# Three f16 products in place of an f32 product in the second and third feed-forward of a two-layer network

## The chip, the cores and the metric

One core of a Trainium2 chip runs the whole program. The metric is the device time of one execution in microseconds (us). Below, PE is the tensor engine, DVE the vector engine, ACT the scalar engine, POOL the GpSimd engine and SP the engine that issues DMAs.

## What is computed

The input is x, 16 sequences of 256 tokens with 128 channels (4096 tokens), and a context of 16 x 64 tokens with 64 channels. There are six stages, each with a residual: a causal attention with a cross attention; a gated feed-forward of 512 hidden channels (the first feed-forward); a causal self-attention with 16 heads of 32 and behind it a feed-forward (the second); a cross attention and behind it a feed-forward (the third); a mixture of eight experts, one per token. The second and third feed-forward, which the change is about, are in the reference:

```python
h = jax.nn.gelu(_ln(x_out, ln3_g, ln3_b) @ li2_w + li2_b, approximate=False)
return x_out + h @ li3_w + li3_b
```

li2_w is 128 x 512 and li3_w is 512 x 128. Everything is f32 in the reference.

## The kernel before

The program is written out by hand: every engine has its own list of instructions, and semaphores join them. x, and the stages' results u and xo, stay in the core's memory.

The second and third feed-forward are both `mha_ffn` (L1119), called with the tag `bf` (L2684) and `cf` (L2694). It works in 8 steps (n = 0 to 7) of 512 tokens, each of 4 slots. The tile z is the normalised tokens, zT their transpose, hT the hidden layer, transposed. The profile calls some tiles by the name under which their memory was first given: b_w_wq and b_w_wk are z, b_w_wv is one of the two zT.

- PE, in slot m of step n, makes one hidden product: 128 of the 512 hidden channels for 512 tokens (L1159, f32, 128 x 128 weights against 512 columns), into one of 3 banks. In slots 2 and 3 it makes the closing products of step n - 1 (`tensor_closing`, L1193): for each of 4 blocks of 128 tokens 4 f32 products of 128 columns, 16 in a step. In slot 1 it transposes z of step n + 1 (L1179). All closings of the last step stand behind it.
- ACT applies gelu to each hidden product (L1266) and writes hT in f32; in slot 1 it copies the transposed z out with gain and offset (L1278).
- DVE takes statistics of the tokens of step n + 2 (L150 to L159), normalises them (L187), and adds bias (L1205) and residual (L1211) to the closings of step n - 1. In between stand pieces of the stages on both sides: the last batches of the attention ahead, the first of the attention behind (`before.vector_slot`, `after.vector_slot`).
- POOL raises the variance to the power -0.5 (L170), and does the neighbouring stages' elementwise work. In step 0 of `bf` it splits the cross attention's three weights into f16 halves (L1877, L1879), for which it waits until they are loaded.

In `cf` there is no stage behind; instead the tokens are routed to experts: for step n - 3 PE makes gate logits and counts (L2421 to L2439), DVE the choice (L2372 to L2402), POOL sends the tokens out by indirect DMA.

The first feed-forward and both attentions already use f16 halves: a value v is written as high = f16(v), low = f16(v - high), and a product of two such values as high x high + high x low + low x high. The memory of the first feed-forward's weight halves (`f.parts`) is free once it is done.

`SelfAttention.run` (L1768) and `CrossAttention.run` drive a list of slots s; POOL's part of a slot is `gpsimd_slot(s)`.

## Time and profile before

| | us |
|---|---|
| runs before: median (lowest, highest) of 3 | 1471.27 (1469.37, 1474.41) |
| the profiled execution's own time | 1476.54 |
| its span, first to last instruction | 1474.8 |
| second feed-forward, first transpose to last closing | 986.4 to 1064.0 |
| cross attention, between the two | 1064.0 to 1259.2 |
| third feed-forward, first transpose to last closing | 1259.2 to 1348.2 |
| mean granted PE clock, share of full speed | 0.965 |

A timeline row gives the start, the time from start to end, engine, line, operation, output <- inputs with their sizes, and how often it stands there in a row; in brackets the idle time ahead and who ended it. An f32 matmul leaves two records. A record is longer than the distance to the next record's start, since matmuls are pipelined and ACT and DVE overlap a little from one instruction to the next; what a product costs is the distance between starts.

### The profile page before, as it was taken

The page shows a single profiled execution, that of the slowest core. Times are in us where ns is not written, and L with a number is a line of the kernel's source. Part 1 is how long each engine was busy: PE and PEld are TensorE (multiplying, and loading weights), DVE is VectorE, ACT ScalarE, POOL GpSimd, SP SyncE. Part 2 cuts the span into 40 slices and gives each one's busy share as a digit, 9 for nine tenths or more (in the row PEclk, how much of TensorE's full clock was granted, in tenths as well). Part 3 has the DMA queues.
Part 4 walks back from the last instruction along what each step waited for, and adds up shares of the span by engine and source line. Part 5 has one row for each costly group of instructions (what it writes and reads, how often), then busy time and mean ns, then how long its engine had stood idle before and what let it go on. Part 6 is the DMA issues. An engine that isn't in the chain of part 4 may idle for free.

```text
span 1474.8 us, 42722 instructions
## 1 busy us (share of the span) xinstructions
PE 1348.1 (91%) x17832; PEld 861.7 (58%) x17848; DVE 976.7 (66%) x2238; ACT 845.1 (57%) x1309; POOL 650.9 (44%) x1118
## 2 busy tenths in 40 slices
PE   6899999987999998999999999988999999898695
PEld 3455555554455544556666666656767777576584
DVE  5788888775554555678888887644568876775132
ACT  2577777766666656466666666543456665431231
POOL 3455555532010013256566655433347775345155
PEclk9999999998999999999999999999989999997798
DMA  7000000000600000000000000011001111022351
GB/s 218 3 3 3 3 3 3 3 3 2 164 1 1 1 1 1 1 2 32 30 18 31 17 31 31 17 45 44 1 31 45 46 50 55 30 90 77 120 158 44
DMA packets 54513, 53.76 MB, mean 36 GB/s; under 512 B 9273, under 2 KB 48573, under 8 KB 54066
## 3 DMA queue, kind: packets, MB, share of 16 engines
q1 hardware_dynamic: 50482, 44.24, 9.9%
q0 software_dynamic: 2816, 6.11, 1.2%
q8 instruction: 142, 2.33, 0.7%
q10 hardware_dynamic: 1024, 0.69, 0.2%
q14 instruction: 49, 0.40, 0.1%
HBM read 20.34 MB, written 14.49 MB: 24 GB/s over the span
## 4 chain that ended last, share of the span: by engine, by line
PE 71%; DVE 10%; ACT 5%; issue 4%; DMA 4%; POOL 3%; SPq 3%; POOLq 0%; DVEq 0%; ACTq 0%
PE psum L1510 6%; PE psum L921 4%; PE psum L1193 4%; PE psum L923 4%; PE psum L922 4%; PE psum L1538 3%; PE psum L1159 3%; PE psum L2507 3%; PE psum L2523 2%; SPq L777 2%; DMA a_QT<-a_nmT 2%; DVE b_nm L1594 2%; PE psum L527 2%; DVE a_nm L587 2%; PE psum L1987 2%
## 5 line engine op out<-in xcount | busy, mean ns | idle before, releaser
L1594 DVE TENSOR_REDUCE b_nm<-psum 128x4 f16<-128x1024 f32 x128 | 157.5, 1231 | 70.2 <-PE psum L1515 69.2
L702 ACT ACTIVATE a_prob<-psum 128x768 f32<-128x768 f32 (+1 forms) x160 | 136.1, 853 | 63.1 <-PE psum L464 61.4
L587 DVE TENSOR_REDUCE a_nm<-psum 128x4 f16<-128x1024 f32 (+1 forms) x96 | 117.3, 1223 | 42.9 <-PE psum L494 30.2
L754 POOL TENSOR_SCALAR_AFFINE_SELECT a_prob<-a_prob 128x512 f32<-128x512 f32 x128 | 81.9, 640 | 124.7 <-ACT a_prob L702 124.5
L170 POOL TENSOR_TENSOR f_ln_rstd<-f_ln_tmp,pow_half 128x4 f32<-128x4 f32 x24 | 25.4, 1057 | 204.2 <-DVE f_ln_tmp L159 204.1
L1049 ACT ACTIVATE xo_sb<-psum,f_w_h_s 128x512 f32<-128x512 f32 x64 | 44.0, 688 | 87.7 <-PE psum L923 87.7
L1510 PE MATMUL psum<-b_QTh,b_KTh 32*128 32x256 f16 x512 | 71.1, 272 | 11.7 <-DVE b_nm L1594 8.5
L1515 PE MATMUL psum<-b_KTh,b_QTh 32*128 32x256 f16 x512 | 70.7, 273 | 1.2 <-DVE b_nm L1594 1.2
L1510 PE MATMUL psum<-b_QTh,b_KTl 32*128 32x256 f16 x512 | 70.1, 268 | 0.0
L1510 PE MATMUL psum<-b_QTl,b_KTh 32*128 32x256 f16 x512 | 70.1, 267 | 0.0
L1515 PE MATMUL psum<-b_KTh,b_QTl 32*128 32x256 f16 x512 | 69.5, 268 | 0.0
L1515 PE MATMUL psum<-b_KTl,b_QTh 32*128 32x256 f16 x512 | 69.4, 268 | 0.0
L1716 POOL TENSOR_SCALAR_AFFINE_SELECT b_late<-f_hT1l 128x256 f32<-128x256 f32 x64 | 28.2, 463 | 88.7 <-ACT f_hT1l L1679 88.7
L2617 POOL DMA_INDIRECT out_dram<-m_ys,m_number x40 | 39.8, 995 | 55.0 <-DVE m_ys L2558 45.3
L990 DVE TENSOR_TENSOR f_hT1l<-xo_sb,f_hT1h 128x512 f16<-128x512 f32 x32 | 22.2, 693 | 49.3 <-ACT f_hT1h L1050 49.3
L921 PE MATMUL psum<-f_hT0h,f_h_wh 128*128 128x512 f16 x128 | 49.3, 385 | 4.6 <-DVE f_hT0l L984 4.5
L990 DVE TENSOR_TENSOR f_hlastl<-xo_sb,f_hlasth 128x512 f16<-128x512 f32 x32 | 22.2, 693 | 45.4 <-ACT f_hlasth L1050 45.4
L1510 PEld LDWEIGHTS psum<-b_QTh,b_KTh 32*128 32x128 f16 x512 | 25.4, 92 | 45.4 <-issue 27.8
L923 PE MATMUL psum<-f_hT0h,f_h_wl 128*128 128x512 f16 x128 | 49.2, 384 | 0.0
L922 PE MATMUL psum<-f_hT0l,f_h_wh 128*128 128x512 f16 x128 | 49.1, 384 | 0.0
L1522 PE MATMUL psum<-b_nmT,b_group_row 32*128 32x256 f16 x512 | 49.1, 268 | 0.0
L1679 ACT ACTIVATE f_hT0h<-psum 128x1024 f32<-128x1024 f32 x32 | 32.7, 1023 | 28.2 <-PE psum L1522 28.2
(448 smaller groups left out, 4642.8 us busy)
## 6 DMA issues: line engine op xcount, KB each, us to landing
f_h_wh<-b_rden SPq DMA_DIRECT2D x64, 128.0 KB, 2.1
f_h_wh<-c_rden SPq DMA_DIRECT2D x64, 128.0 KB, 2.1
expert_in<-empty SPq DMA_DIRECT2D x8, 662.5 KB, 10.9
m_xt<-expert_in SPq DMA_DIRECT2D x8, 662.5 KB, 5.0
m_w<-in_L_ffn_w_dram SPq DMA_DIRECT2D x16, 256.0 KB
x_sb<-in_x_dram SPq DMA_DIRECT2D x8, 256.0 KB, 4.7
f_w_h_w<-in_L_ffn_h_w_dram SPq DMA_DIRECT2D x2, 1024.0 KB, 7.4
out_dram<-m_send SPq DMA_DIRECT2D x8, 256.0 KB, 2.5
```

Of the source, the lines that this page charges most:

```text
L587: nc.vector.tensor_reduce(out, psum[:, banks, :].rearrange("p i (a b) -> p i a b", a=groups), X, ALU.max, negate=True).then_inc(max_done, 1)
L702: nc.scalar.activation(prob[unit % 5][:, :, 0:width], psum[:, first:first + 2, 0:width], ACT.Exp, scale=SCALE).then_inc(exp_done, 1)
L754: nc.gpsimd.affine_select(out=diagonal, in_=diagonal, compare_op=ALU.is_ge, fill=0.0, base=0, pattern=[[0, 4], [1, P]], channel_multiplier ...
L921: nc.tensor.matmul(bank, wh[:, k, m * P:m * P + P], xh[:, k, :], start=(k == 0), stop=False)
L922: nc.tensor.matmul(bank, wh[:, k, m * P:m * P + P], xl[:, k, :], start=False, stop=False)
L923: inst = nc.tensor.matmul(bank, wl[:, k, m * P:m * P + P], xh[:, k, :], start=False, stop=(k == K4 - 1))
L990: nc.vector.tensor_tensor(out[1][:, m, :], whole[m % 2], out[0][:, m, :], ALU.subtract).then_inc(low_done, 1)
L1193: inst = nc.tensor.matmul(bank[:, to], hT[n % 2][:, k, to], li3[:, k, :], start=(t == 0 and k == 0), stop=True, skip_group_check=True)
L1510: t.matmul(psum[:, first_bank + i, to], key[r, g, own], q[r, g, :], start=(k + first + second == 0), stop=False, skip_group_check=True)
L1515: inst = t.matmul(psum[:, 2 + i, to], q[r, g, own], key[r, g, :], start=(k + first + second == 0), stop=(first == 1), skip_group_check=True)
L1522: inst = t.matmul(psum[:, first_bank + i, k * T:k * T + T], self.group_row[r, g, :], self.nmT[n % 2][r, :], start=False, stop=True, skip_g ...
L1594: v.tensor_reduce(self.nm[:, :, :].rearrange("p t (j r) -> p j t r", r=32)[:, 2 * e:2 * e + 2, :, g], self.pr.psum[:, 2:4, :].rearrange("p ...
```

## The change

In `bf` both layers become three products of f16 halves; in `cf` only the first does, and the closings stay f32. The weights are split once by POOL, by a new class whose four (`bf`) or two (`cf`) instructions are put ahead of slots 40, 44, 48 and 52 of the self-attention and 40 and 44 of the cross attention; the halves lie in the memory of the first feed-forward's. ACT writes the transposed z twice, in f32 and in f16, and the low half is subtracted by POOL in `bf` and by DVE in `cf`. In `bf` ACT also applies gelu twice, into an f32 tile `whole` (2 of them) and into the f16 high half, and DVE subtracts (`vector_low`). The f32 zT has one buffer now, the f16 halves have two.

```diff
+class Halves:
+    def gpsimd_half(self, i):
+        g, (whole, high, low) = self.nc.gpsimd, self.parts[i // 2]
+        if i == 0:
+            self.w.arrived(g)
+        if i % 2 == 0:
+            g.tensor_copy(high, whole).then_inc(self.done, 1)
+        else:
+            g.wait_ge(self.done, i)
+            g.tensor_tensor(low, whole, high, ALU.subtract).then_inc(self.done, 1)
...
+    def tensor_hidden(n, m):
+        u, cols, bank = 4 * n + m, slice(m * P, m * P + P), psum[:, (4 * n + m) % 3, :]
+        if m == 0:
+            nc.tensor.wait_ge(zT_out, n + 1)
+        if u == 0:
+            nc.tensor.wait_ge(halves.done, halves.all)
+        if u >= 3:
+            nc.tensor.wait_ge(act_done, u - 2)
+        nc.tensor.matmul(bank, li2[0][:, cols], zTh[n % 2][:, :], start=True, stop=False)
+        nc.tensor.matmul(bank, li2[1][:, cols], zTh[n % 2][:, :], start=False, stop=False)
+        if m == 0:
+            nc.tensor.wait_ge(zT_low, n + 1)
+        nc.tensor.matmul(bank, li2[0][:, cols], zTl[n % 2][:, :], start=False, stop=True).then_inc(full, 1)
...
@@ tensor_closing
+            if split:
+                nc.tensor.wait_ge(low_done, 4 * (n + 1))
+        for k in range(K4 if split else 0):
+            for x, y in ((hTh, li3h), (hTh, li3l), (hTl, li3h)):
+                inst = nc.tensor.matmul(bank[:, to], x[n % 2][:, k, to], y[:, k, :], start=(t == 0 and k == 0 and x is hTh and y is li3h),
+                                        stop=True, skip_group_check=True)
...
+    def vector_low(n, m):
+        nc.vector.wait_ge(act_done, 4 * n + m + 1)
+        nc.vector.tensor_tensor(hTl[n % 2][:, m, :], whole[m % 2][:, :], hTh[n % 2][:, m, :],
+                                ALU.subtract).then_inc(low_done, 1)
+
+    def tokens_low(engine, n):
+
+        engine.wait_ge(zT_out, n + 1)
+        engine.tensor_tensor(zTl[n % 2][:, :], zT[:, :], zTh[n % 2][:, :], ALU.subtract).then_inc(zT_low, 1)
...
@@ scalar_hidden
+        if split:
+            if n or m >= 2:
+                nc.scalar.wait_ge(low_done, 4 * n + m - 1)
+            nc.scalar.activation(whole[m % 2][:, :], bank, ACT.Gelu, bias=bias)
+            nc.scalar.activation(hTh[n % 2][:, m, :], bank, ACT.Gelu, bias=bias).then_inc(act_done, 1)
...
@@ scalar_program
+                    if n >= 0:
+                        nc.scalar.wait_ge(zT_low, n + 1)
+                    for to in (zT, zTh[(n + 1) % 2]):
+                        inst = nc.scalar.activation(to[:, :], psum[:, 3, :], ACT.Identity, bias=w["cols"][:, 1, :],
+                                                    scale=w["cols"][:, 0, :])
+                    inst.then_inc(zT_out, 1)
```

Where the new instructions stand in each engine's list matters. The rows below are the engines' lists, one line per instruction or run of equal ones, for three places.

DVE in step 2 of `bf`. Before, from the residual of step 0 to that of step 1:

```order
L1205 TENSOR_TENSOR bf_res<-psum,bf_w_b3 128x512
L1211 TENSOR_TENSOR u_sb<-u_sb,bf_res 128x512
L150 BN_STATS f_ln_stat<-xo_sb 128x6 x4
L154 BN_AGGR f_ln_mv<-f_ln_stat 128x2 x4
L159 TENSOR_SCALAR f_ln_tmp<-f_ln_mv 128x4
L187 TENSOR_SCALAR b_w_wq<-xo_sb,f_ln_mv,f_ln_rstd 128x128 x4
L1205 TENSOR_TENSOR bf_res<-psum,bf_w_b3 128x512
```

And now:

```order
L1264 TENSOR_TENSOR bf_hTl1<-bf_whole0,bf_hTh1 128x512
L1264 TENSOR_TENSOR bf_hTl1<-bf_whole1,bf_hTh1 128x512
L1244 TENSOR_TENSOR bf_res<-psum,bf_w_b3 128x512
L1250 TENSOR_TENSOR u_sb<-u_sb,bf_res 128x512
L150 BN_STATS f_ln_stat<-xo_sb 128x6 x4
L154 BN_AGGR f_ln_mv<-f_ln_stat 128x2 x4
L159 TENSOR_SCALAR f_ln_tmp<-f_ln_mv 128x4
L1264 TENSOR_TENSOR bf_hTl0<-bf_whole0,bf_hTh0 128x512
L1264 TENSOR_TENSOR bf_hTl0<-bf_whole1,bf_hTh0 128x512
L187 TENSOR_SCALAR b_w_wq<-xo_sb,f_ln_mv,f_ln_rstd 128x128 x4
L1264 TENSOR_TENSOR bf_hTl0<-bf_whole0,bf_hTh0 128x512
L1264 TENSOR_TENSOR bf_hTl0<-bf_whole1,bf_hTh0 128x512
```

Two of a step's four subtractions came between the statistics and the normalisation, two between the normalisation and the residual.

POOL at the start of `bf`, around the split of the cross attention's weights (c_wq, c_wk, c_wv). Before:

```order
L170 TENSOR_TENSOR f_ln_rstd<-f_ln_tmp,pow_half 128x4 x3
L1877 CAST c_wqh<-c_w_wq 128x512
L1879 TENSOR_TENSOR c_wql<-c_w_wq,c_wqh 128x512
L1877 CAST c_wkh<-c_w_wk 64x512
L1879 TENSOR_TENSOR c_wkl<-c_w_wk,c_wkh 64x512
L1877 CAST c_wvh<-c_w_wv 64x512
L1879 TENSOR_TENSOR c_wvl<-c_w_wv,c_wvh 64x512
L170 TENSOR_TENSOR f_ln_rstd<-f_ln_tmp,pow_half 128x4
L1740 TENSOR_TENSOR u_sb<-u_sb,xo_sb 128x256
```

And now, from the second power on:

```order
L1270 TENSOR_TENSOR bf_zTl0<-b_w_wv,bf_zTh0 128x512
L170 TENSOR_TENSOR f_ln_rstd<-f_ln_tmp,pow_half 128x4
L1270 TENSOR_TENSOR bf_zTl1<-b_w_wv,bf_zTh1 128x512
L1951 CAST c_wqh<-c_w_wq 128x512
L1953 TENSOR_TENSOR c_wql<-c_w_wq,c_wqh 128x512
L1951 CAST c_wkh<-c_w_wk 64x512
L1953 TENSOR_TENSOR c_wkl<-c_w_wk,c_wkh 64x512
L1951 CAST c_wvh<-c_w_wv 64x512
L1953 TENSOR_TENSOR c_wvl<-c_w_wv,c_wvh 64x512
L170 TENSOR_TENSOR f_ln_rstd<-f_ln_tmp,pow_half 128x4
L1270 TENSOR_TENSOR bf_zTl0<-b_w_wv,bf_zTh0 128x512
```

The low half of the third step's zT (the last row) now stands behind the split and one more power.

DVE in a routed step of `cf`, ahead of the residual. Before:

```order
L2401 COPY m_send1<-m_token 128x4
L2402 TENSOR_TENSOR m_row_u1<-m_place,m_own 128x4
L187 TENSOR_SCALAR b_w_wq<-xo_sb,f_ln_mv,f_ln_rstd 128x128 x4
L1205 TENSOR_TENSOR cf_res<-psum,cf_w_b3 128x512
L2357 TENSOR_TENSOR m_send0<-x_sb,cf_res 128x4x128
```

And now:

```order
L2477 COPY m_send1<-m_token 128x4
L2478 TENSOR_TENSOR m_row_u1<-m_place,m_own 128x4
L187 TENSOR_SCALAR b_w_wq<-xo_sb,f_ln_mv,f_ln_rstd 128x128 x4
L1270 TENSOR_TENSOR cf_zTl1<-b_w_wv,cf_zTh1 128x512
L1244 TENSOR_TENSOR cf_res<-psum,cf_w_b3 128x512
L2433 TENSOR_TENSOR m_send0<-x_sb,cf_res 128x4x128
```

The subtraction of the tokens' low half came in just ahead of the residual; the very first one, for step 0, stands ahead of the reciprocal of the attention's last sums (L2068).

## Rows read from the trace of the kernel before

**Rows 1.** the page: busy time by engine; the chain that ended last, by engine
```profile
PE 1348.1 (91%) x17832; PEld 861.7 (58%) x17848; DVE 976.7 (66%) x2238; ACT 845.1 (57%) x1309; POOL 650.9 (44%) x1118
...
PE 71%; DVE 10%; ACT 5%; issue 4%; DMA 4%; POOL 3%; SPq 3%; POOLq 0%; DVEq 0%; ACTq 0%
```

**Rows 2.** windows, steps 3 to 6 of the second feed-forward: length, busy by engine, clock, DMA
```profile
1020.16:1027.60 7.44, 7.44 (x46) 5.48 (x45) 4.48 (x19) 3.36 (x5) 1.95 (x3) 1.00 0.01 2
1027.60:1035.05 7.45, 7.45 (x47) 5.49 (x45) 5.21 (x17) 3.36 (x5) 2.45 (x3) 1.00 0.00 0
1035.05:1042.49 7.44, 7.44 (x46) 5.48 (x45) 5.40 (x25) 3.36 (x5) 3.66 (x7) 1.00 0.00 0
1042.49:1050.27 7.78, 7.78 (x49) 5.77 (x48) 2.63 (x7) 4.95 (x9) 2.51 (x5) 1.00 0.01 2
```

**Rows 3.** timeline of PE in step 4: start, length, engine, line, operation, count
```profile
1029.76 1.02 PE L1159 MATMUL psum<-b_w_wv,bf_w_li 128*128 128x512 f32 x2
1030.62 1.95 PE L1193 MATMUL psum<-bf_w_li,bf_hT 128*128 128x128 f32 x16
1032.40 1.02 PE L1159 MATMUL psum<-b_w_wv,bf_w_li 128*128 128x512 f32 x2
```

**Rows 4.** timeline of PE in the first feed-forward, f16 products of 512 and of 128 columns
```profile
392.37 0.22 PE L948 MATMUL psum<-f_w_wh,f_hlasth 128*128 128x128 f16 x1
...
393.20 0.22 PE L948 MATMUL psum<-f_w_wh,f_hlasth 128*128 128x128 f16 x1
...
555.26 0.38 PE L921 MATMUL psum<-f_hT0h,f_h_wh 128*128 128x512 f16 x1
555.48 0.38 PE L922 MATMUL psum<-f_hT0l,f_h_wh 128*128 128x512 f16 x1
```

**Rows 5.** timeline of ACT in step 6 of the second feed-forward
```profile
1045.00 0.77 ACT L1278 ACTIVATE bf_zT<-psum,bf_w_cols 128x512 f32<-128x512 f32 x1
...
1045.71 0.69 ACT L1266 ACTIVATE bf_hT<-psum,bf_w_b 128x512 f32<-128x512 f32 x1
...
1046.30 0.44 ACT L2104 ACTIVATE c_cTw<-psum,c_w_by,c_w_gy 64x128 f32<-64x128 f32 x1
```

**Rows 6.** a subtraction to f16 of 128x512 on DVE (min/median/max ns), and one on POOL
```profile
L990 DVE TENSOR_TENSOR f_hT1l<-xo_sb,f_hT1h x32: 691/693/694, 372.3 to 604.7; 128x512 f16<-128x512 f32 x32
...
1009.31 1.15 POOL L1879 TENSOR_TENSOR c_wvl<-c_w_wv,c_wvh 64x512 f16<-64x512 f32 x1
```

**Rows 7.** timeline of DVE and POOL, normalisation beside POOL's work, and without it
```profile
1024.37 1.12 DVE L187 TENSOR_SCALAR b_w_wk<-xo_sb,f_ln_mv,f_ln_rstd 128x128 f32<-128x128 f32 x4 [1.19 <-POOL f_ln_rstd L170]
...
1031.71 0.72 POOL L2154 TENSOR_TENSOR c_zi<-c_zi,c_w_g 128x256 f32<-128x256 f32 x1
1031.84 1.99 DVE L187 TENSOR_SCALAR b_w_wq<-xo_sb,f_ln_mv,f_ln_rstd 128x128 f32<-128x128 f32 x4 [0.71 <-POOL f_ln_rstd L170]
```

**Rows 8.** timeline of POOL and PE at the second feed-forward's early stop
```profile
1010.42 1.01 POOL L170 TENSOR_TENSOR f_ln_rstd<-f_ln_tmp,pow_half 128x4 f32<-128x4 f32 x1
...
1012.71 0.78 PE L1179 MATMUL psum<-ident,b_w_wk 128*128 128x128 f32 x4 [2.29 <-DVE b_w_wk L187]
```

**Rows 9.** timeline of the third feed-forward: ACT and PE in step 4, DVE at its end
```profile
1299.48 0.60 ACT L2449 ACTIVATE m_zT<-psum 128x512 f32<-128x512 f32 x1 [1.53 <-PE psum L2413]
...
1300.24 0.40 PE L2421 MATMUL psum<-m_gate_b,ones 1*128 1x32 f32 x2
...
1309.47 0.69 DVE L1205 TENSOR_TENSOR cf_res<-psum,cf_w_b 128x512 f32<-128x512 f32 x1 [1.42 <-PE psum L1193]
```

**Rows 10.** timeline of the third feed-forward's start: DVE, PE, PE's wait for a load
```profile
1262.61 1.75 DVE L2068 RECIPROCAL c_rden<-psum 128x256 f32<-128x256 f32 x1
...
1269.03 1.08 PE L1179 MATMUL psum<-ident,b_w_wq 128*128 128x128 f32 x4 [2.19 <-DVE b_w_wq L187]
...
1288.15 0.38 PE L2421 MATMUL psum<-m_gate_b,ones 1*128 1x32 f32 x2 [0.98 <-DMA m_gate_b<-in_L_ffn_gate_b_dram]
```

**Rows 11.** waits in the self-attention: engine, tile, line, releaser, total us, times, longest
```profile
POOL b_late L1716 <- ACT f_hT1h L1679: 20.3, 19, 1.8
```

More of the change, by code:

```diff
@@ L214, in __getitem__, with __init__ @@
         return self.tiles[name]
+class Halves:
+    def __init__(self, pr, w, tag, parts):
+        self.nc, self.w, self.parts, self.all = pr.nc, w, parts, 2 * len(parts)
+        self.done = pr.sem(tag + "_half")
+    def gpsimd_half(self, i):
[7 more added lines that the diff above has]
+            g.tensor_tensor(low, whole, high, ALU.subtract).then_inc(self.done, 1)
 class Ring:
@@ L1153, in tensor_program @@
                 if 0 <= n < NB:
-                    u = 4 * n + slot
-                    if slot == 0:
-                        nc.tensor.wait_ge(zT_ready, n + 1)
-                    if u >= 3:
-                        nc.tensor.wait_ge(act_done, u - 2)
-                    nc.tensor.matmul(psum[:, u % 3, :], li2[:, slot * P:slot * P + P], zT[n % 2][:, :], start=True,
-                                     stop=True).then_inc(full, 1)
+                    tensor_hidden(n, slot)
                 if last_slot(n, slot) is not None:
@@ L1191, in tensor_closing @@
                 nc.tensor.wait_ge(before.num_out, 2 * B)
-        for k in range(K4):
+            if split:
[4 more added lines that the diff above has]
+                                        stop=True, skip_group_check=True)
+        for k in range(0 if split else K4):
             inst = nc.tensor.matmul(bank[:, to], hT[n % 2][:, k, to], li3[:, k, :], start=(t == 0 and k == 0),
@@ L1247, in vector_program @@
                 routing.vector_second(n - 3)
+            lows = range(K4) if split and 0 <= n < NB else []
             vector_next(n, (0,))
+            for m in lows[0:1]:
+                vector_low(n, m)
             if n == NB:
@@ L1251, in vector_program @@
             vector_next(n, (1,))
+            for m in lows[1:2]:
+                vector_low(n, m)
             if 0 <= n + 2 < NB:
@@ L1254, in vector_program @@
             vector_next(n, (2,))
+            for m in lows[2:4]:
+                vector_low(n, m)
             if n == 0 and routing:
                 routing.vector_prepare()
+            if routing and 0 <= n + 1 < NB:
+                tokens_low(nc.vector, n + 1)
             if 0 <= n - 1 < NB - 1:
@@ L1265, in scalar_hidden @@
             nc.scalar.wait_ge(y_full, n - 1)
[L1266 to L1267 removed]
+        bank, bias = psum[:, (4 * n + m) % 3, :], w["b2"][:, m:m + 1]
+        if split:
+            if n or m >= 2:
+                nc.scalar.wait_ge(low_done, 4 * n + m - 1)
+            nc.scalar.activation(whole[m % 2][:, :], bank, ACT.Gelu, bias=bias)
+            nc.scalar.activation(hTh[n % 2][:, m, :], bank, ACT.Gelu, bias=bias).then_inc(act_done, 1)
+        else:
+            nc.scalar.activation(hT[n % 2][:, m, :], bank, ACT.Gelu, bias=bias).then_inc(act_done, 1)
     def scalar_program():
@@ L1293, in gpsimd_program @@
                 ln.gpsimd_rstd(n + 2)
+            if not routing and 0 <= n + 1 < NB:
+                tokens_low(nc.gpsimd, n + 1)
             if n == 0:
@@ L1778, in run @@
                 self.pr.clear_old()
+            if s in self.SPLIT:
+                self.next_halves.gpsimd_half(self.SPLIT.index(s))
             self.gpsimd_slot(s)
@@ L2213, in run @@
                 self.pr.clear_old()
+            if s in self.SPLIT:
+                self.next_halves.gpsimd_half(self.SPLIT.index(s))
             self.gpsimd_slot(s)
```

35 lines of the change are left out of this document (23 added, 12 removed).

## The prediction

> **What bounds the kernel now.** I read the page first. PE is busy for 91% of the span and makes 71% of the chain that ended last; no other engine makes more than 10% [rows 1]. So PE work that is taken away is time gained, where PE is the engine that is waited for, and the question is whether it stays so in the two stretches that the change touches. The second feed-forward (bf) lasts 77.6 us, the third (cf) 89 us.
>
> Next the windows of bf by step. In steps 3, 4 and 5 PE is busy for the whole 7.44 us at full clock, DVE for 4.48, 5.21 and 5.40, ACT for 3.36; step 6 takes 7.78, with 4.95 of ACT [rows 2]. These steps are PE's alone. Then the timelines, for the price of each product, read as the distance between starts. An f32 product of 512 columns takes 0.86 (from 1029.76 to 1030.62), sixteen records of the closings, which are eight products of 128 columns, take 1.78, so 0.223 each [rows 3].
>
> **What the change does to PE.** The first feed-forward shows the f16 prices: 0.216 between two products of 512 columns (555.26 to 555.48), and 0.83 for 15 products of 128 columns (392.37 to 393.20), so 0.055 each [rows 4]. Three of them cost 0.65 and 0.166. A hidden product saves 0.21, a closing product 0.056. For one step of bf PE falls by 4 x 0.21 + 16 x 0.056 = 1.74, to 5.7; for one of cf by 0.85. If PE alone mattered, 8 x 1.74 + 8 x 0.85 = 20.7 us would go. Most of that will not be seen.
>
> **What it adds.** ACT gets four more gelus and one more copy per step of bf. Gelu to next instruction is 0.59, copy to gelu 0.71 [rows 5]. So ACT's step is 8 x 0.59 + 2 x 0.71 = 6.14, above PE's 5.7. DVE gets four subtractions per step. Their like, f32 minus f16 to f16, takes 0.69 [rows 6]; as a DVE instruction overlaps the next by nearly 0.1, I add 0.61 each, 2.44 per step. POOL gets one subtraction of 1.15 per step [rows 6], which is hidden as such, since POOL is busy for only 2 to 3.7 of a step [rows 2].
>
> Steps 3 to 5 of bf. DVE's work becomes 4.48 + 5.21 + 5.40 + 3 x 2.44 = 22.4, against the 22.3 that the three steps take now. DVE takes PE's place, and nothing is gained. There is also a loss. Where POOL ran elementwise work beside it, the normalisation took 1.99, and 1.12 where not [rows 7]. POOL's new subtraction stands right behind the power for which the normalisation waits, so the two will run together. Two of the three steps don't have this cost yet, which is 0 to 1.7 in all; I take the middle, 0.9, since only part of the 1.15 need coincide. With it and the 0.1 above: **+1.0**.
>
> The Trainium skill has a rule for that which speaks against the change: "SBUF — State Buffer", section "Who interferes with whom", says that DVE and POOL share a pair of ports under an exclusive lock, and that a DVE instruction with two SBUF inputs also contends with a POOL instruction that reads SBUF. By it DVE's own subtractions, not the normalisation alone, could be held for a whole POOL instruction. The 1.99 agrees; that a subtraction is held, no row here shows. It is a rival below.
>
> The early stop of bf, in steps 1 and 2. POOL splits the cross attention's weights until 1010.42, then takes the power of step 3, and only then can DVE normalise; PE waits 2.29 until 1012.71 [rows 8]. That stop stays, as a load and POOL set it. Now POOL's subtraction of step 2 stands behind the same power, and the first hidden product of step 2 needs it: 1010.42 + 1.01 + 1.15 = 1012.6. So the two hidden products that PE made before the stop now lie behind it, and what PE saved ahead of it is lost. Behind the stop DVE has two subtractions of step 1 between the normalisation and the residual, and two of step 2 ahead of the gelu that needs their buffer: 4 x 0.61, of which PE's lower work covers about half. I take **+1.3**, bounds 0 and 2.4.
>
> Step 6 of bf. ACT has the cross attention's copies there: 4.95 + 4 x 0.59 + 0.71 = 8.0 against 7.78, so +0.25 at least. The gelu of `whole` waits for the subtraction two back, and that one for DVE; one such wait costs up to a subtraction and a gelu more. I take **+1.0**, bounds 0.25 and 2.3.
>
> Step 7 and the closings behind it. No statistics and no normalisation are left on DVE, so PE counts again: 1.74 + 16 x 0.056 = **-2.6**, bounds -3.3 and -1.5.
>
> bf in sum: 1.0 + 1.3 + 1.0 - 2.6 = **+0.7**.
>
> cf. ACT gets one copy, DVE one subtraction per step, and the closings stay. At the start the first subtraction stands ahead of the reciprocal at 1262.61, and everything on DVE behind it is some 0.7 late, the third step's transposes too, which now start at 1269.03 [rows 10]. PE gets that back by step 2, and in any case it stops at 1288.15 for the gate weights, whose load waits for the last batch of the attention [rows 10]. So steps 0 to 2 give 0. From there on: the first product of a step only fills the time until ACT has copied the routed tokens (1299.48 + 0.60, PE goes on at 1300.24 [rows 9]), and its 0.21 turns into a wait. The other three save 0.64 per step. DVE allows it: it waits 1.42 for PE at the end of the step [rows 9], and of this 0.61 goes to the subtraction, which leaves 0.8. Steps 3 to 6 give 4 x 0.64 = 2.6; step 7, where DVE's choice ends last, gives one product, 0.2: **-2.8**, bounds -3.4 and -0.5.
>
> The split weights: 2 CASTs and 2 subtractions of POOL in the self-attention, one pair in the cross attention, one instruction in a slot. POOL waits for ACT by up to 1.8, about 1.1 at a time (20.3 in 19 waits) [rows 11]. I take 0, bounds 0 and +1.
>
> The sum is 0.7 - 2.8 = -2.1. Against the profiled execution's own 1476.54 that is 1474.4. This execution lies 5.3 above the median of the runs, 1471.27, and from that the forecast is **1469.2**. A measurement of this kernel can tell about 0.3%, 4.4 us, from no change; this is within it.
>
> **The rivals.** First, DVE keeps up (faster). Its subtractions fill gaps that it has anyway, and ACT's 6.14 becomes the step: steps 3 to 5 give 3 x 1.3 = 3.9, step 6 +0.25, the early stop +0.6, the end -2.6, cf -2.8: -8.5, 1462.8. For it speaks that DVE's busy time holds waits of the port kind, as the 1.99; against it that DVE takes its list in order, and that each subtraction waits for a gelu.
>
> Second, the shared port decides (slower). POOL's subtraction holds DVE for its full 1.15 in each of steps 2 to 6, and the cross attention's POOL pieces hold the subtractions too: 5 x 1.15 less the 0.9 already counted is 4.9, so bf is at +5.6. In cf DVE's subtraction comes beside POOL's descriptors, its margin of 0.8 is used up, and the gain falls to 0.5. That is +5.1, 1476.4. It decides from the point at which DVE's step is longer than PE's 5.7, which by the sum above it is.
>
> Third, the gain in cf is swallowed by DVE alone and bf goes as forecast: +0.5, 1471.8, no change.
>
> **How the numbers follow.** The forecast has 0.48, DVE keeping up 0.25, the port 0.22, the third 0.05. The predicted time is the forecast's. The range goes from 1462.8, the first rival's value, rounded to 1463, to 1477, just past the second's: what lies outside it is about half of each of the first two rivals' spread around their values, some 0.2. Faster by over 0.3% is the first rival, 0.25; slower the second, 0.22; the forecast and the third lie between, 0.53.
>
> **What would show it.** In the windows of bf's steps 3 to 5: PE busy well below the step (near 5.7 of 7.4 to 7.9), DVE near full. ACT's `whole` gelus should be released by DVE's subtractions, not by PE. The normalisations near 2 us in most steps. The early stop should end at 1012.6 with a hidden product, not a transpose. In cf a routed step should take 9.8 in place of 10.43, with a longer PE wait ahead of L2421. I am wrong if bf's steps come down to 6.5 (then DVE's sum is at fault), if they reach 9 (then the port), or if the cross attention, whose PE work is unchanged, changes its length by more than 1 us.

## The result, and the profile after

The changed kernel takes 1479.34 us (median of 16 runs, 1474.51 to 1484.27), the kernel before, run beside it, 1473.43 (16 runs, 1464.09 to 1490.16). The medians lie 5.9 apart. The ratio of the two kernels' runs is 1.0049, with a 95% interval of 1.0032 to 1.0066: slower by 7 us, by 4.7 at the least. The profiled execution took 1482.5, its span is 1480.6; before, 1476.54 and 1474.8.

To see where, I cut the span at four instructions that both kernels have. "bf" is from bf's first transpose to DVE's first maxima of the cross attention (c_nm), "cross attention" from there to cf's first transpose, "cf" to DVE's last cf_res. One profile shows one execution: for the cross attention and cf a difference of 2 us is within what profiles of unchanged code differ by.

| stretch | before | changed | difference |
|---|---|---|---|
| up to bf | 986.40 | 986.75 | +0.35 |
| bf | 79.06 | 82.86 | +3.80 |
| cross attention | 193.70 | 195.23 | +1.53 |
| cf | 91.46 | 90.98 | -0.48 |
| the rest | 124.18 | 124.78 | +0.60 |

The page of the changed kernel, busy time by engine and the chain by engine, against [rows 1]:

```profile
PE 1330.6 (90%) x18024; PEld 848.7 (57%) x18040; DVE 1009.2 (68%) x2278; ACT 872.1 (59%) x1357; POOL 672.4 (45%) x1132
...
PE 59%; DVE 17%; POOL 7%; issue 5%; ACT 5%; DMA 3%; SPq 3%; POOLq 0%; DVEq 0%; ACTq 0%
```

PE lost 17.5 us of work and 12 points of the chain (of 71). DVE and POOL have taken 7 and 4 of these.

Windows of bf in the changed kernel. The first three go from the fifth transpose to the sixth and so on to the eighth, and stand for steps 3, 4 and 5; the last goes from there, in step 6, to the first maxima. The columns are those of [rows 2]: length, busy time of PE, of PE's weight loads, of DVE, ACT and POOL, then PE's granted clock and the DMA.

```profile
1023.12:1030.48 7.36, 6.08 (x66) 4.10 (x65) 6.89 (x20) 6.18 (x10) 2.50 (x2) 1.00 0.00 1
1030.48:1039.58 9.10, 6.24 (x65) 4.07 (x64) 8.96 (x26) 6.18 (x10) 5.63 (x6) 1.00 0.01 2
1039.58:1047.58 8.00, 6.10 (x65) 4.11 (x65) 7.83 (x26) 6.28 (x10) 3.62 (x5) 1.00 0.00 0
1047.58:1069.61 22.03, 18.25 (x299) 14.71 (x298) 18.25 (x45) 14.28 (x26) 11.96 (x17) 0.92 0.01 3
```

The three steps took 7.44, 7.45 and 7.44 before, all of it PE. Now they take 7.36, 9.10 and 8.00. PE is busy for 6.1 to 6.2 in each, DVE for 6.89, 8.96 and 7.83: DVE is the bound. The last stretch took 21.25 before.

The second of these steps as a timeline of ACT, POOL, DVE and PE:

```profile
1034.72 0.80 ACT L1345 ACTIVATE bf_zTh<-psum,bf_w_cols 128x512 f16<-128x512 f32 x1
1035.06 1.03 POOL L170 TENSOR_TENSOR f_ln_rstd<-f_ln_tmp,pow_half 128x4 f32<-128x4 f32 x1 [2.23 <-DVE f_ln_tmp L159]
1036.07 1.64 POOL L1270 TENSOR_TENSOR bf_zTl<-b_w_wv,bf_zTh 128x512 f16<-128x512 f32 x1
1036.61 2.92 DVE L187 TENSOR_SCALAR b_w_wq<-xo_sb,f_ln_mv,f_ln_rstd 128x128 f32<-128x128 f32 x4
1037.76 0.39 PE L1187 MATMUL psum<-bf_zTl,f_w_wh 128*128 128x512 f16 x1 [0.88 <-POOL bf_zTl L1270]
1039.58 0.66 PE L1212 MATMUL psum<-ident,b_w_wq 128*128 128x128 f32 x4 [0.79 <-DVE b_w_wq L187]
1040.24 0.69 ACT L1328 ACTIVATE bf_whole<-psum,bf_w_b 128x512 f32<-128x512 f32 x1 [1.64 <-DVE bf_hTl L1264]
```

POOL's subtraction takes 1.64 and the normalisation beside it 2.92. Before, this step's normalisation took 1.99, and one with nothing beside it on POOL 1.12 [rows 7]. PE waits for both, and the `whole` gelu for DVE, as forecast.

The early stop, where PE waited 2.29 [rows 8]:

```profile
1011.35 1.01 POOL L170 TENSOR_TENSOR f_ln_rstd<-f_ln_tmp,pow_half 128x4 f32<-128x4 f32 x1
1012.33 1.16 POOL L1270 TENSOR_TENSOR bf_zTl<-b_w_wv,bf_zTh 128x512 f16<-128x512 f32 x1
...
1013.54 0.61 PE L1187 MATMUL psum<-bf_zTl,f_w_wh 128*128 128x512 f16 x1 [4.23 <-POOL bf_zTl L1270]
```

And a stop in step 6 that the kernel before did not have, with what PE does behind it:

```profile
1050.83 0.60 DVE L187 TENSOR_SCALAR c_z<-u_sb,c_lnx_mv,c_lnx_rstd 128x128 f32<-128x128 f32 x2
...
1051.48 0.69 PE L1972 MATMUL psum<-ident,c_z 128*128 128x128 f32 x2 [2.62 <-DVE c_z L187]
1052.17 0.31 PE L1229 MATMUL psum<-f_w_wh,bf_hTh 128*128 128x128 f16 x1
1052.28 0.31 PE L1229 MATMUL psum<-f_w_wl,bf_hTh 128*128 128x128 f16 x1
```

DVE's four subtractions of the step stand in part ahead of the cross attention's normalisation. Behind the stop a product of 128 columns starts 0.11 after the last, not 0.055: PE's granted clock is 1.2 GHz there for some 3 us after the stop, and the window's mean clock is 0.92 instead of 1.00.

The start of cf on DVE and PE, against [rows 10]:

```profile
1267.26 1.11 DVE L187 TENSOR_SCALAR b_w_wk<-xo_sb,f_ln_mv,f_ln_rstd 128x128 f32<-128x128 f32 x4 [1.12 <-POOL f_ln_rstd L170]
1268.29 0.68 DVE L1270 TENSOR_TENSOR cf_zTl<-b_w_wv,cf_zTh 128x512 f16<-128x512 f32 x1
1269.03 0.61 PE L1187 MATMUL psum<-cf_zTl,f_w_wh 128*128 128x512 f16 x1 [0.65 <-DVE cf_zTl L1270]
...
1273.18 2.08 DVE L187 TENSOR_SCALAR b_w_wq<-xo_sb,f_ln_mv,f_ln_rstd 128x128 f32<-128x128 f32 x4 [1.19 <-POOL f_ln_rstd L170]
...
1276.27 1.10 DVE L1270 TENSOR_TENSOR cf_zTl<-b_w_wv,cf_zTh 128x512 f16<-128x512 f32 x1
1277.42 0.61 PE L1187 MATMUL psum<-cf_zTl,f_w_wh 128*128 128x512 f16 x1 [3.30 <-DVE cf_zTl L1270]
```

The third of the three products for a step's first 128 hidden channels waits for a subtraction that stands behind the normalisation of the step after, and behind the preparation of the routing. The windows of cf, first to fifth transpose and from there to the last cf_res:

```profile
1264.84:1299.70 34.86, 27.36 (x152) 19.12 (x153) 25.21 (x89) 16.39 (x24) 11.03 (x14) 0.80 0.10 26
1299.70:1355.82 56.12, 52.73 (x398) 43.82 (x396) 43.68 (x208) 21.51 (x33) 31.43 (x29) 1.00 0.28 91
```

The same two before, 31.87 and 59.59:

```profile
1259.16:1291.03 31.87, 27.72 (x138) 18.46 (x139) 23.88 (x94) 14.13 (x20) 12.05 (x15) 0.92 0.12 36
1291.03:1350.62 59.59, 58.19 (x380) 46.99 (x378) 39.80 (x197) 19.24 (x29) 29.01 (x28) 0.95 0.25 82
```

So cf loses 3.0 at its start and wins 3.5 behind it. Most of the 3.5 is not the products. These are the windows from the last transpose to the last cf_res: before, changed, and cf_alone_mended, a kernel described below that has the same instructions in cf:

```profile
1323.27:1350.62 27.35, 25.95 (x176) 21.89 (x174) 15.22 (x75) 7.21 (x11) 11.39 (x11) 0.94 0.19 65
```

```profile
1330.28:1355.82 25.54, 23.28 (x182) 19.97 (x180) 16.23 (x77) 7.79 (x12) 11.86 (x12) 1.00 0.23 78
```

```profile
1321.65:1348.82 27.17, 24.91 (x182) 21.59 (x180) 16.23 (x77) 7.79 (x12) 11.87 (x12) 0.94 0.22 74
```

At the same mean clock of 0.94 the f16 products are worth 0.2 here; the other 1.6 come with a clock of 1.00. In the same way the step behind the fifth transpose took 11.39 before at 0.91 and 10.40 now at 1.00; unchanged code at 1.00 took 10.42 too (in bf_alone). At a like clock two steps of 0.3 and 0.36 and the 0.2 are left, some 0.9 in all.

### The profile page after: what moved, and what is told of

Read it like the earlier page. It is cut to its first block, busy times and chain, and to the rows that moved or that the text cites. A ratio compares the mean times of both kernels' runs of the same rounds, so it can differ in the third digit from the quotient of the medians.

```text
span 1480.6 us, 43236 instructions
## 1 busy us (share of the span) xinstructions
PE 1330.6 (90%) x18024; PEld 848.7 (57%) x18040; DVE 1009.2 (68%) x2278; ACT 872.1 (59%) x1357; POOL 672.4 (45%) x1132
## 4 chain that ended last, share of the span: by engine, by line
PE 59%; DVE 17%; POOL 7%; issue 5%; ACT 5%; DMA 3%; SPq 3%; POOLq 0%; DVEq 0%; ACTq 0%
PE psum L1581 6%; PE psum L939 4%; PE psum L940 4%; PE psum L941 4%; PE psum L1609 3%; PE psum L2583 2%; PE psum L2599 2%; SPq L795 2%; DMA a_QT<-a_nmT 2%; DVE c_nm L2114 2%; DVE b_nm L1665 2%; PE psum L545 2%; DVE a_nm L605 2%; PE psum L1593 2%; DVE c_rden L2142 1%
```

## The experiments

Each kernel was timed beside the kernel before. The ratios are to that, with their 95% intervals, which are about ±0.2%, 3 us. Two kernels that differ by less than that are not told apart. The stretches come from one profile each. bf repeats well: unchanged it took 79.06, 78.92 and 78.93, changed 82.86, 82.94 and 82.83.

### Each stage alone

cf_alone:

```diff
-                bf_halves = Halves(pr, bf, "bf", ...)
+                bf_halves = None
```

> Only the third feed-forward (cf) has its first layer as three f16 products; the second (bf) is as before, without its weight halves. Stage by stage the changed kernel against the one before stands at: +0.35 at the start of bf, +3.5 in bf, +1.5 in the cross attention, -0.5 in cf (+4.4 in its first three steps, -4.9 in the rest), +0.6 behind. If these add up (theory of the stages), this kernel keeps the +1.5 of the cross attention, where POOL splits cf's weights, and the -0.5 of cf: about +1 against before, +0.1%, and cf's third transpose comes 4.4 later than its first did. Rival: the +1.5 in the cross attention is a phase that the late bf leaves behind, then it is gone here and the kernel stands at -0.5 to 0. Rival of my forecast: cf's start costs nothing, -2.8.

bf_alone:

```diff
-                    cf_halves = Halves(pr, cf, "cf", ...)
+                    cf_halves = None
```

> Only bf is changed, cf is as before, no split of cf's weights in the cross attention. Theory of the stages: +0.35 + 3.5 = +3.8 at the end of bf; if POOL's split of cf's weights makes the cross attention's +1.5, the total stays at +3.8 to +4.4 (+0.3%). Rival: the +1.5 is a phase that bf leaves behind, then the total is +5.5 to +6. By my forecast bf would be at +0.7.

Measured: cf_alone 1.0020 (1.0003 to 1.0038), bf_alone 1.0038 (1.0022 to 1.0055). The two add up to the whole, 0.58% against 0.49%, and each part of the change loses by itself. For bf the place is settled by that: +3.9 in its stretch. For cf and the cross attention it is not, since their stretches vary: cf with unchanged code took 91.46 in one profile and 88.03 in another. Both losses lie above the middle of what was expected, 0.1% and 0.3%. bf_alone's 5.6 us are nearer to the rival, by which the late bf also delays the cross attention, but the interval, 3.2 to 8.1, holds both.

### What holds bf

no_vector_low takes DVE's four subtractions a step away, and with them PE's and ACT's waits for them; the low half is then a copy of the high one, and ACT and PE do as much work as in the changed kernel:

```diff
-            lows = range(K4) if split and 0 <= n < NB else []
+            lows = []
...
-            nc.scalar.activation(whole[m % 2][:, :], bank, ACT.Gelu, bias=bias)
+            nc.scalar.activation(hTl[n % 2][:, m, :], bank, ACT.Gelu, bias=bias)
```

> As changed, but DVE's four subtractions of bf's hidden layer are left out: the first gelu writes the low half's tile itself (f16, so the low half is wrong), PE and ACT work as in the changed kernel, POOL's subtraction of the tokens' low half stays. Theory, DVE's list bounds bf's steps 3 to 6: they fall from 7.4, 9.1, 8.0 to ACT's 6.14 to 6.6 each, the stretch from the first transpose to the cross attention's first maxima falls from 82.9 to 76 to 78, the whole is 4 to 7 faster than the changed kernel. Rival, POOL's late low half beside the normalisation bounds them: the steps stay above 7.2 and the stretch above 80.5.

Measured: bf 73.44, the whole 0.9980 (0.9960 to 0.9999). Its windows and one of its normalisations:

```profile
1023.86:1029.56 5.70, 5.70 (x65) 4.32 (x64) 4.40 (x17) 5.70 (x11) 2.16 (x2) 1.00 0.00 0
1029.56:1036.74 7.18, 6.05 (x65) 4.03 (x64) 6.33 (x21) 7.18 (x13) 4.50 (x6) 1.00 0.01 3
1036.74:1042.89 6.15, 5.93 (x65) 4.18 (x65) 5.44 (x22) 5.12 (x9) 2.99 (x5) 1.00 0.00 0
```

```profile
1033.85 2.84 DVE L187 TENSOR_SCALAR b_w_wq<-xo_sb,f_ln_mv,f_ln_rstd 128x128 f32<-128x128 f32 x4 [0.71 <-POOL f_ln_rstd L170]
```

The normalisations are as long as in the changed kernel (1.87 to 2.84), POOL's subtraction is there, and still the first step takes 5.70, which is PE's own work; the second is ACT's, busy for all of its 7.18. In the first step a DVE that is held by POOL costs nothing, as it has slack. My bounds, 76 to 78, were too high: bf fell by 9.4, and the whole by 10 us, not by 4 to 7.

no_tokens_low takes POOL's subtraction away, and PE's and ACT's waits for it; ACT writes a second copy of the high half in its place:

```diff
-            if not routing and 0 <= n + 1 < NB:
-                tokens_low(nc.gpsimd, n + 1)
...
-                    for to in (zT, zTh[(n + 1) % 2]):
+                    for to in (zTl[(n + 1) % 2] if split else zT, zTh[(n + 1) % 2]):
```

> As changed, but POOL's subtraction of bf's tokens is left out: ACT writes the low tile itself (f16, wrong by that), PE does all its products. Theory of DVE's list: the normalisations fall from 1.87 to 1.12, the powers from 1.39 to 1.02, so DVE's step falls by 0.8 and PE's wait for the low half goes; steps 3 to 6 come to 7.2 to 7.6 each, the stretch of bf from 82.9 to 80 to 81, the early stop ends 1 to 1.5 earlier. Rival, the low half and the port are the whole trouble: the stretch falls below 79 (the kernel before). If neither matters: 82.5 or more.

Measured: bf 78.53, the whole 1.0022 (1.0002 to 1.0041). Windows of the same three steps:

```profile
1021.48:1027.18 5.70, 5.70 (x65) 4.32 (x64) 5.19 (x21) 5.62 (x10) 1.51 (x2) 1.00 0.00 0
1027.18:1034.61 7.43, 6.20 (x65) 4.03 (x64) 7.33 (x22) 6.18 (x10) 4.39 (x5) 1.00 0.01 3
1034.61:1041.77 7.16, 6.26 (x65) 4.10 (x65) 6.99 (x26) 6.03 (x10) 2.77 (x4) 1.00 0.00 0
```

DVE's work in the three falls from 23.68 to 19.51. The three normalisations make 2.4 of that (6.74 to 4.31); another 1.3 is one subtraction and one bf_res that fell inside the three windows there and outside them here. I had expected 80 to 81, and had put below 79 down to the rival, that POOL's subtraction is the whole trouble. With no_vector_low beside it, it is not: bf falls to 73.4 without DVE's subtractions and to 78.5 without POOL's. DVE's list alone leaves bf about where it was before (78.5 against 79.1), and the 3.8 of loss comes with POOL's subtraction on top of a full DVE.

low_on_vector gives that subtraction to DVE, ahead of the normalisation. In cf it stands ahead of the normalisation too, as in cf_low_early below:

```diff
+            if 0 <= n + 1 < NB:
+                tokens_low(nc.vector, n + 1)
             if 0 <= n + 2 < NB:
                 vector_normed(n + 2, 1)
...
-            if not routing and 0 <= n + 1 < NB:
-                tokens_low(nc.gpsimd, n + 1)
```

> As changed, but the tokens' low half is made by DVE in both feed-forwards, ahead of the normalisation; POOL's subtraction in bf is gone. What tells apart: if the shared port is what POOL's subtraction costs bf (normalisation 1.87 instead of 1.12, power 1.39 instead of 1.02: 0.75 and more a step), DVE pays 0.61 a step and wins 0.75, the early low half frees the first product, and bf's stretch falls from 82.9 to 80 to 82 (without the subtraction at all it was 78.5). If only DVE's list counts, its sum grows by 0.61 less 0.75: unchanged steps of 7.4 to 9, 82.5 to 83.5. cf as in cf_low_early: 87 to 88.5. The whole: 2 to 4 faster than the changed kernel, still no faster than before.

Measured: bf 81.36, the whole 1.0028 (1.0005 to 1.0050). Here DVE does 0.61 a step more than in no_tokens_low, and has normalisations of 1.11; bf is still 1.5 shorter than in the changed kernel. In steps 3 to 5 the normalisations give back 2.4 and the three subtractions take 2.05, so the same instruction costs DVE a little less in its own list than on POOL beside it. The low half also comes earlier here, and how much of the 1.5 is due to that was not told apart; in the whole the two kernels can't be told apart.

closings_only and bf_first_only each keep one of bf's two layers in halves. The list of weights to split is cut to one, and the other layer's code is that of the kernel before:

```diff
-                bf_halves = Halves(pr, bf, "bf", [(li2 and its halves), (li3 and its halves)])
+                bf_halves = Halves(pr, bf, "bf", [(li2 and its halves)])
```

(this is bf_first_only; closings_only keeps li3 instead.)

> As changed, but bf's first layer stays one f32 product; the closings are three f16 products with two gelus and DVE's subtractions. PE's step is 7.44 less 0.9, 6.55. Theory of DVE's list: the normalisations are at 1.12 again, the step is DVE's 4.5 to 5.4 and 2.44, 7.0 to 7.8, and the stretch of bf is 79.5 to 81, slower than before by 0.5 to 2. Rival, without POOL's subtraction DVE keeps up: steps 6.6, stretch below 78.

> As changed, but bf's closings stay f32: one gelu, no subtractions of the hidden layer, so ACT and DVE work as before but for one copy; PE takes 6.6 a step; the tokens' low half stays on POOL behind the power. Theory that DVE's four subtractions are the trouble of bf: steps 3 to 6 fall to 6.6 to 7.0, bf gains about 2 to 3.5 against the kernel before, and the whole is 5 to 7 faster than the changed one. Rival, the late low half and the shared port: POOL's subtraction beside the normalisation still holds the first product of each step, steps stay at 7.4 and more, bf stays at +1 or worse, and the whole is 2 to 3 faster than the changed one.

Measured: closings_only bf 79.61, 1.0024 (1.0003 to 1.0045); bf_first_only bf 78.40, 0.9992 (0.9973 to 1.0011). bf_first_only's windows:

```profile
1020.29:1026.89 6.60, 6.60 (x50) 5.37 (x49) 5.23 (x20) 3.94 (x7) 3.07 (x4) 1.00 0.01 2
1026.89:1033.48 6.59, 6.59 (x49) 5.37 (x48) 5.77 (x18) 3.93 (x7) 3.57 (x4) 1.00 0.00 0
```

PE is the bound again, its step 0.85 shorter, and DVE has 0.8 to 1.4 of slack. The first layer's split is one POOL subtraction and one copy of ACT a step, and pays in these steps; the closings' split is four subtractions of DVE and four gelus, and does not. The whole is 8 us faster than the changed kernel, a little more than the 5 to 7 expected. Against the kernel before, bf wins 0.7 and not the 2 to 3.5 expected, and the whole nothing that can be told from zero. The first four distances between transposes take it back, 38.26 against 35.48: at the early stop PE waits 5.23 for the low half in this kernel, 2.29 in the kernel before.

```profile
1010.42 0.61 PE L1193 MATMUL psum<-bf_zTl,f_w_wh 128*128 128x512 f16 x1 [5.23 <-POOL bf_zTl L1276]
```

### cf: the low half earlier, and the split weights

cf_low_early moves one line:

```diff
+            if routing and 0 <= n + 1 < NB:
+                tokens_low(nc.vector, n + 1)
             if 0 <= n + 2 < NB:
                 vector_normed(n + 2, 1)
...
-            if routing and 0 <= n + 1 < NB:
-                tokens_low(nc.vector, n + 1)
```

> As changed, but in cf DVE makes the tokens' low half ahead of the normalisation of the step after, not behind it and the preparations. Theory: the first hidden product of steps 0 and 1 waits 0.65 and 3.30 for that subtraction, which stands behind a normalisation that itself waits for POOL; ahead of it, it can run as soon as ACT has copied (1273.26 instead of 1276.27). cf's third transpose then comes 2.5 to 3.3 earlier, and the kernel is 2.5 faster than the changed one (-0.17%). Rival: PE's start is bound by the loads of the gate weights (my forecast), then what is won at the start is lost again at the first gate product, and the end moves by less than 0.5.

Measured: the whole 1.0045 (1.0026 to 1.0064), against 1.0049 of the changed kernel; the 2.5 us expected are within what two such intervals allow, and not shown by them. The profile shows its place:

```profile
1269.36 0.69 DVE L1270 TENSOR_TENSOR cf_zTl<-b_w_wv,cf_zTh 128x512 f16<-128x512 f32 x1 [0.41 <-ACT cf_zTh L1345]
1270.14 2.08 DVE L187 TENSOR_SCALAR b_w_wq<-xo_sb,f_ln_mv,f_ln_rstd 128x128 f32<-128x128 f32 x4
```

The wait of 3.30 is gone, and cf's third transpose comes 10.55 after its first, not 14.26 (before: 9.87). Over all profiles, the time from cf's first to its fifth transpose is 29.4 to 31.9 with f32 products (3 profiles), 33.1 to 35.2 with the low half late (7), 29.6 to 31.6 with it early (6). From the first to the third transpose it is plainer: 9.87 with f32 products in all three, 13.5 to 14.3 with the low half late, 10.3 to 10.6 with it early. The clock does not decide it (9.87 at 1.00 in the kernel before and at 0.83 in bf_alone, 13.46 at 0.87 in cf_alone). So the late low half costs 3 to 4 us at its place.

split_in_bf joins bf_first_only and the early low half (that is first_only_early), and moves the split of cf's weights:

> In bf only the first layer is split (closings f32, one gelu), in cf DVE makes the tokens' low half ahead of the normalisation. It joins the kernels bf_first_only and cf_low_early. In the profiles bf_first_only's bf took 78.4 (before 79.06), cf_low_early's cf 86.9 (with the late low half 89.1 to 91.0). If they add: 2 to 3 faster than bf_first_only, so 0.2 to 0.3% below the kernel before, with the cross attention's +1.5 for the split of cf's weights still in it. Rival: what the early low half wins is lost at the gate weights' load, then no difference from bf_first_only, within 0.1% of before.

```diff
+            if later and n in (3, 4):
+                later.gpsimd_half(n - 3)
...
-                    c_stage.next_halves = cf_halves
+                    c_stage.next_halves = None
```

> first_only_early with POOL's two instructions on cf's first-layer weights (0.61 and 1.16) moved from the cross attention's slots 40 and 44 into bf's steps 3 and 4. In all eight profiles with them in the cross attention, the distance between the sixth and seventh maxima is 12.8 to 13.3 (once 15.4), in the two without them 12.0 and 11.8. Theory: that is their price, the distance falls to 11.7 to 12.0, bf stays at 76.7 to 78.4, and the whole is 1 to 1.5 faster than first_only_early. Rival: the next batches have slack and take it back, or the cost only moves into bf; then the sixth distance falls and the whole stays.

Measured: first_only_early 0.9985 (0.9969 to 1.0002), 1 us below bf_first_only where 2 to 3 were expected; split_in_bf 0.9991 (0.9970 to 1.0013), where 1 to 1.5 less than first_only_early was expected. The sixth and seventh maxima in the changed kernel, and POOL's two pieces between them:

```profile
1132.08 2.35 DVE L2114 TENSOR_REDUCE c_nm<-psum 128x16 f16<-128x1024 f32 x2
1144.85 2.34 DVE L2114 TENSOR_REDUCE c_nm<-psum 128x16 f16<-128x1024 f32 x2
```

```profile
1137.33 0.61 POOL L228 CAST f_w_wh<-cf_w_li 128x512 f16<-128x512 f32 x1
...
1143.43 1.16 POOL L231 TENSOR_TENSOR f_w_wl<-cf_w_li,f_w_wh 128x512 f16<-128x512 f32 x1
```

and in split_in_bf, which has no such pieces there:

```profile
1123.38 2.35 DVE L2122 TENSOR_REDUCE c_nm<-psum 128x16 f16<-128x1024 f32 x2
1134.93 2.35 DVE L2122 TENSOR_REDUCE c_nm<-psum 128x16 f16<-128x1024 f32 x2
```

12.77 against 11.55. In all ten profiles with the pieces the distance is 12.8 to 13.4 (once 15.4), in the six without them 11.6 to 12.0. That is the price at the place, some 1.3 us. In the whole it does not show. The cross attention varies by more (below), and the rival of this run is in part true: some of the cost moves into bf. Beside the second of the moved pieces a normalisation of bf takes 3.70, where it took 2.85 in first_only_early, and from bf's fifth transpose to the maxima split_in_bf takes 0.65 longer (41.15 and 40.50).

```profile
1030.44 3.70 DVE L187 TENSOR_SCALAR b_w_wq<-xo_sb,f_ln_mv,f_ln_rstd 128x128 f32<-128x128 f32 x4 [0.71 <-POOL f_ln_rstd L170]
```

cf_alone_mended leaves bf as it was before the change and has both mends in cf, the early low half and the moved split of its weights:

> bf as before the change; cf's first layer as three products, the tokens' low half ahead of the normalisation, cf's weights split in bf's steps 3 and 4. Against cf_alone (+0.2%) it takes away the two costs named: 2.5 to 3 at cf's start, 1.3 in the cross attention. Theory: 3.5 to 4 faster than cf_alone, so -0.1% against before (cf at 87 to 88.5, bf at 79). Rival: cf's start is set by the gate weights' load and the self-made order matters for nothing: as cf_alone, +0.1 to +0.2%.

Measured: 0.9984 (0.9966 to 1.0003), 0.36% below cf_alone, a little more than expected. With both mends cf's part of the change is no loss any more; a gain is not shown.

### The early stop

stop_removed and its two controls move the split of the cross attention's weights on POOL one step later:

```diff
-            if n == 0 and after:
+            if n == 1 and after:
                 for i in range(3):
                     after.gpsimd_split(i)
```

> split_in_bf, and the cross attention's weights are split by POOL in bf's step 1, behind the power of step 3 and the low half of step 2, instead of in step 0 ahead of both. Nothing needs these halves before bf's step 6. Theory: the early stop (2.3 of PE before the change, 4.2 with it) goes, since POOL no longer waits for the load of the weights ahead of the power; the first four distances of bf's transposes, 36.2 to 38.3 in sum, fall by 3 to 4, the whole by 3 to 4, so 0.4 to 0.5% under the kernel before. Rival: the last batches of the self-attention set these steps (they carry its tail), then the sum falls by less than 1.

> The changed kernel with the cross attention's weights split in bf's step 1 behind the power and the low half, nothing else. In the changed kernel the first hidden product of step 2 waits 4.23 for that low half. Theory: the stop goes, but DVE, which bounds bf here and stood idle for 7.06 in that stop, keeps its list; bf's first four distances fall from 36.4 by 2 to 4, bf's stretch from 82.9 to 79 to 81, and the whole is 2 to 4 faster than the changed one: about as before the change. Rival: DVE's list bounds the stretch as a whole, the stop only covers DVE's arrears, then less than 1.

> The kernel before, with that same move alone. If stop_removed owes its 0.53% to the move and not to the f16 products: this kernel is 3 to 5 faster than before (-0.2 to -0.35%), bf's first four distances fall from 35.5 to 31.5 to 32.5. If the f16 first layers make it worth more (PE's 0.85 a step is only free once nothing else stops it): this kernel gains less than 3, and stop_removed stands 4 to 6 below it.

Measured: stop_removed (on split_in_bf) 0.9947 (0.9926 to 0.9969), bf 73.15; changed_split_later (on the changed kernel) 1.0041 (1.0022 to 1.0059), bf 79.30; before_split_later (on the kernel before) 0.9968 (0.9952 to 0.9985), bf 74.89. Windows of stop_removed's bf, from the third transpose to the sixth:

```profile
1002.32:1008.92 6.60, 6.60 (x51) 5.38 (x49) 3.23 (x5) 3.43 (x6) 4.27 (x5) 1.00 0.30 92
1008.92:1015.51 6.59, 6.59 (x49) 5.28 (x48) 4.78 (x15) 3.93 (x7) 5.53 (x6) 1.00 0.00 1
1015.51:1022.11 6.60, 6.60 (x50) 5.37 (x49) 5.26 (x20) 3.94 (x7) 2.69 (x3) 1.00 0.01 2
```

The stop goes in all three. stop_removed beats the kernel before by 0.53%, 7.8 us, but 0.32% of it is the moved split alone, which has nothing to do with f16. The f16 first layers are worth the difference, some 0.2% (the two intervals overlap, so this is likely rather than shown), and bf is 1.7 shorter for them. On the changed kernel the move wins 3.6 in bf, as expected, but the whole falls by 0.08%, 1 us, where 2 to 4 were expected. Its profile's cf took 93.78, with a clock of 0.94 behind the fifth transpose; whether the runs lost the rest there is not shown.

### Why the stretches behind bf vary

The first three distances between maxima in the cross attention sum to 38.6 at a mean clock of 0.87 in the changed kernel, to 34.6 at 1.00 in no_vector_low, with the same code. Windows of the two:

```profile
1069.61:1108.16 38.55, 34.43 (x689) 23.18 (x690) 26.21 (x65) 23.23 (x45) 17.67 (x32) 0.87 0.09 29
```

```profile
1061.98:1096.61 34.63, 30.21 (x690) 21.04 (x690) 25.95 (x65) 23.04 (x45) 17.68 (x32) 1.00 0.10 33
...
1287.93:1346.55 58.62, 55.83 (x398) 46.54 (x396) 43.58 (x208) 21.51 (x33) 31.44 (x29) 0.94 0.27 87
```

cf behind its fifth transpose is the same list in all kernels with f16 there: 56.0 to 56.8 in six profiles with a clock of 0.97 to 1.00, 58.5 to 58.8 in seven with 0.94. The same stop can be followed by a stretch at 1.2 GHz or not: just behind the first maxima PE stands still for 2.0 to 2.4 in all 16 profiles, and the granted clock falls in it or right after it in 14 of them, in the kernel before too, and in two (no_vector_low and first_only_early) it does not. In the two places above such stretches cost 1 to 4 us. That is more than most of the terms here, and one profile shows only one draw of it. Whether a change makes a drop likelier was not tested.

## Why the prediction was wrong

It said -2.1 in the sum and "same"; measured is +7, and 1479.34 is outside the range of 1463 to 1477. Two steps of it had the wait wrong (the end of bf, the start of cf), and one price was too small (POOL beside the normalisation).

**PE's prices and the turn to DVE: right.** PE's step fell to 6.1, in no_vector_low to 5.70; the `whole` gelus are released by DVE, the normalisations take 1.9 and more.

**bf steps 3 to 5, +1.0: mechanism right, size off.** Three steps took 24.46 where the sum gave 23.3, so the change cost 2.1. The term for the normalisations held by POOL was too small: 0.9 was taken, with 1.7 as the most, since one of the three already took 1.99 and was thought to be paid for. They took 1.87, 2.92 and 1.95 where they had taken 1.12, 1.99 and 1.12, which is 2.5 in all; the one already held was held once more. On top come 0.8 in which DVE waits, for gelus and powers: a sum of an in-order engine's work is a floor. Against these, the windows hold only 11 of the 12 subtractions and a little less of the neighbouring stages, so that DVE's busy time, 23.68, is only 0.4 above the sum. That the sum of DVE's work came so near was in part luck.

**The early stop, +1.3: about right.** The first four distances rose by 0.9. It ended at 1013.54, not 1012.6, as the weights' load was issued 1.3 later. bf began 0.35 later, and the normalisation of 989.17, beside POOL's first subtraction, took 2.03 in place of 1.11; DVE's reciprocal of the self-attention, on which the copy ahead of the load depends, stands behind it.

**Step 6 and the end, +1.0 and -2.6: the step that failed.** Together -1.6 was forecast, and from the last transpose to the maxima it came to +0.78. I wrote that with no statistics and normalisation left "PE counts again". DVE has the cross attention's first pieces there, and its four subtractions stand among them: PE waits 2.62 for c_z, for which it did not wait before, and 1.16 for bf_res (0.88 before), and goes on at 1.2 GHz for some 3 us. Without the subtractions (no_vector_low) PE waited 1.41 for c_z and this stretch took 19.09, 2.16 less than before; so PE's gain was there, and the subtractions took 2.9 of it.

**cf's start, 0: the second step that failed.** I argued that PE stops for the gate weights at 1288.15 in any case, so a late start would be hidden. But their load is issued behind the last batch of the attention, whose last additions stand on DVE behind the same late work: PE's first gate product came 9.7 later too (5.7 of that is the later start of cf), and the stop fell only from 0.98 to 0.31. A wait that looks like a fixed date was relative to the start. I had costed what the subtraction delays behind it on DVE, not what it delays itself: it stood behind a normalisation and the preparation, and PE's third product waited 3.30 for it. Cost: 3 to 4 us, by the late and early kernels above.

**cf's later steps, -2.8: the number by luck.** The profile has -3.5, of which 2.6 come with the clock, as the windows above show; at a like clock some 0.9 is left. Steps fell by 0.36 (10.42 to 10.06), not 0.64. The wait ahead of the gate product came as forecast: there 0.41 lie between two starts (1327.97 and 1328.38), not 0.216. The missing 0.28 went to a second wait, for DVE's choice of the expert (m_carry). The forecast had looked for DVE's slack at the end of a step alone, where 0.28 to 0.53 of the 1.42 is left.

```profile
1331.72 0.41 PE L2512 MATMUL psum<-m_hot,m_earlier 128*128 128x32 f32 x2 [0.20 <-DVE m_carry L2460]
```

**The split weights, 0: nearly.** In the self-attention nothing shows (+0.35 up to bf). In the cross attention the pieces cost 1.3 where they stand; in the changed kernel POOL works there from 1136.79 to 1144.6 without a wait. I had read POOL's waits for the self-attention alone.

**The rivals.** DVE keeping up was wrong for the change, though right for bf_first_only. The shared port had the right sign and came nearest (1476.4 against 1479.34, and +5.6 for bf against +3.8). That it was near in the whole is in part luck: it priced nothing at the start of cf, where 3 us went, and took 4.9 for POOL's subtraction, where each normalisation of steps 3 to 5 lost 0.75 to 0.93. The Trainium skill's rule, "SBUF — State Buffer", section "Who interferes with whom", that of DVE and POOL the one that has the shared ports blocks the other for the whole of its instruction, agrees with the rows: beside DVE's subtractions, which have two inputs in SBUF, POOL's power took 1.38 in place of 1.01, and beside POOL's subtraction DVE's normalisation took 1.87 in place of 1.12. There the first of its four instructions took 1.10, the others 0.33, and it ended 0.1 after POOL's (1029.63 and 1029.55). By its exclusive lock alone I would have expected no_vector_low to suffer as well; its normalisations did, its steps did not. What decides there is whether DVE has slack.

**The check by the cross attention's length** (within 1 us) was no check: it varies from 189.7 to 197.7 over 16 profiles. Its first three distances alone vary from 34.6 to 38.7, with the clock.

## What to carry to other kernels

Splitting an f32 product into f16 halves moves work from PE to the engines that make the low halves; split only as far as they keep slack, here the layer with one subtraction a step and not the one with four. Place each low half by when its reader needs it, ahead of anything that itself waits, and don't excuse a delay by a later stop before asking whether what ends that stop is issued behind the same delay. Before buying PE time, remove the stops: one moved split was worth 0.32%, the f16 first layers of two stages some 0.2% on top of it, and without it nothing that could be measured. And before a gain or loss of one profile is put down to a change, compare stretches at a like clock.
